# The attention batch of a two-layer block scheduled anew on one Trainium2 core: a third bank for maxima, other banks for the products with values

## The reference

```python
qkv = (x @ w_qkv).reshape(Bx, Tx, 3, H, HD)          # H = 16 heads, HD = 16
q, k, v = ...                                         # each [B, H, T, HD]
scores = jnp.einsum('bhqd,bhkd->bhqk', q, k) * SCALE
scores = jnp.where(causal[None, None], scores, -jnp.inf)
geo_bias = q_proj[..., :, None] * k_proj[..., None, :]
scores = scores + head_scales[None, :, None, None] * geo_bias
attn = jax.nn.softmax(scores, axis=-1)
out = jnp.einsum('bhqk,bhkd->bhqd', attn, v)
return out.transpose(...).reshape(Bx, Tx, Cx) @ w_out
```

## Time and profile before

| | |
|---|---|
| median of three runs | 2681.28 us |
| profiled execution | 2683.27 us, span 2681.3 us |
| mean granted clock of TensorE, whole span | 0.925 |
| TensorE matmuls | 2320.9 us busy, 87% of the span |
| VectorE | 1624.2 us, 61% |
| ScalarE | 1314.3 us, 49% |
| GpSimd | 435.1 us, 16% |
| attention, first to last score product | about 1100 us to 2149 us of the span |

### The profile page before, as it was taken

One profiled execution on the slowest core, in us unless ns is written; L12 is line 12 of the kernel. 1 busy time (PEld: TensorE's weight loads), 2 busy tenths in 40 slices (PEclk: granted clock), 3 DMA queues, 4 the chain that ended last, 5 costly groups with the idle time before them and its releaser, 6 DMA issues. The chain is left out here.

```text
span 2681.3 us, 45165 instructions
## 1 busy us (share of the span) xinstructions
PE 2320.9 (87%) x15010; PEld 1680.5 (63%) x15010; DVE 1624.2 (61%) x3570; ACT 1314.3 (49%) x2260; POOL 435.1 (16%) x364
## 2 busy tenths in 40 slices
PE   7999999998799996588888888888888875169997
PEld 6666667666688884455555555555555565158996
DVE  4666767675444546656666666665666555766664
ACT  3565656564445554555555554555555543034442
POOL 0000000000111114210000000000000022046664
PEclk8999999999899997799989998999999987579998
DMA  4300000000000001232222222332222128145542
GB/s 113 110 0 0 0 0 0 0 0 17 15 0 0 0 0 39 50 81 76 77 71 74 72 73 70 73 76 71 72 72 72 38 92 280 47 130 123 127 93 32
DMA packets 122975, 156.64 MB, mean 58 GB/s; under 512 B 26896, under 2 KB 104096, under 8 KB 122784
## 3 DMA queue, kind: packets, MB, share of 16 engines
q1 hardware_dynamic: 104480, 129.85, 17.7%
q0 software_dynamic: 14336, 25.44, 4.9%
q10 hardware_dynamic: 4096, 0.53, 0.1%
HBM read 96.26 MB, written 58.98 MB: 58 GB/s over the span
## 5 line engine op out<-in xcount | busy, mean ns | idle before, releaser
L1386 DVE TENSOR_REDUCE at_top<-psum 128x1 f32<-128x512 f32 (+3 forms) x1024 | 456.7, 484 | 346.9 <-PE psum L1122 346.6
L1567 ACT ACTIVATE out_x<-psum 128x512 f32<-128x512 f32 (+1 forms) x768 | 385.4, 536 | 449.5 <-PE psum L1140 448.1
L1120 PE MATMUL psum<-out_x 96*128 96x512 bf16 (+3 forms) x1024 | 292.9, 312 | 59.5 <-DVE at_top L1386 42.3
L1138 PE MATMUL psum<-out_x 98*128 98x512 bf16 (+3 forms) x1024 | 289.0, 309 | 60.9 <-DMA out_x<-at_neg_top 37.8
L1122 PE MATMUL psum<-at_mask_q,at_ident_b 128*128 128x128 bf16 x1024 | 205.0, 226 | 0.0
L1120 PEld LDWEIGHTS psum<-out_x 96*128 96x128 bf16 x1024 | 102.6, 100 | 162.4 <-DVE at_top L1386 105.1
L1140 PE MATMUL psum<-at_mask_k,at_ident_b 128*128 128x128 bf16 x1024 | 202.5, 224 | 0.0
L1138 PEld LDWEIGHTS psum<-out_x 98*128 98x128 bf16 x1024 | 101.5, 99 | 159.3 <-issue 70.8
L1156 PE MATMUL psum<-out_x,at_values 128*32 128x512 f32 (+3 forms) x2048 | 165.7, 467 | 0.8 <-ACT out_x L1567 0.8
L2360 POOL DMA_INDIRECT out<-ex_result,slot_tokens x64 | 119.5, 1868 | 102.9 <-DVE ex_result L2492 88.3
L1156 PEld LDWEIGHTS psum<-out_x,at_values 128*32 128x32 f32 x2048 | 64.1, 116 | 94.3 <-issue 79.0
(11 more groups left out here) (400 smaller groups left out, 5896.1 us busy)
## 6 DMA issues: line engine op xcount, KB each, us to landing
out_x<-qk_parts SPq DMA_DIRECT2D x128, 192.0 KB
out_x<-qk_parts SPq DMA_DIRECT2D x128, 128.0 KB
qk_parts<-at_q_parts SPq DMA_DIRECT2D x96, 128.0 KB
qk_parts<-at_k_parts SPq DMA_DIRECT2D x96, 128.0 KB
x_residual<-in_x SPq DMA_DIRECT2D x16, 512.0 KB, 3.9
out_x<-qk_parts SPq DMA_DIRECT2D x128, 64.0 KB
token_rows<-ro_h_tok SPq DMA_DIRECT2D x16, 512.0 KB, 3.0
token_rows<-ro_gate_row SPq DMA_DIRECT2D x16, 512.0 KB, 4.1
```

Of the source, the lines that this page charges most:

```text
L1120: pe.matmul(out, q_stack[0:STACK, h, qt * P:(qt + 1) * P], k_stack[0:STACK, h, 0:w], start=True, stop=True)
L1138: pe.matmul(bank(bk)[:, col:col + w], k_stack[0:STACK + N_SHIFT, h, kt * P:(kt + 1) * P], q_stack[0:STACK + N_SHIFT, h, kt * P:T], start=T ...
L1386: dve.tensor_reduce(top[:, h, qt:qt + 1], bank(MAX0 + n % 2)[:, col:col + w], AX.X, ALU.max).then_inc(mxr.sem, 1)
L1567: act.activation(probs[:, slot(h), 512 * f:512 * f + w], bank(f)[:, 0:w], ACT.Exp).then_inc(ex.sem, 1)
```

## The change

Maxima get a bank for each fill (banks 3, 4 and 6), so a fill waits for the same fill of the head before. The products with values and the turned maxima go to the side banks, chosen by group (`PV_BANK`, `TOP_BANK`), turned outputs always to bank 7 (`O_BANK`), and the two output products and the two turnings back take opposite banks (`OUT_BANK`, `DELTA_BANK`). `oT` has two buffers. q and k products come in the order q, k, q, k, one after each of the heads 0 to 3, v products after heads 5 and 11 instead of both after head 3; other side work moves by a head or so. VectorE negates the maxima after the second fill of a head instead of the third. The row DMAs of maxima move from ScalarE's list to SP's (except the very first). SP stores by halves of the heads with a semaphore for each, and interleaves rows, stores and loads. The core of the diff:

```diff
-        MAX0, SIDE_A, PV_BANK, SIDE_B = 3, 5, 6, 7
+        MAX0, SIDE_A, MAX2, SIDE_B = 3, 5, 6, 7
+        PV_BANK = (SIDE_A, SIDE_A, SIDE_A, SIDE_B)
+        TOP_BANK = (SIDE_A, SIDE_B, SIDE_A, SIDE_A)
+        O_BANK = SIDE_B
+        OUT_BANK, DELTA_BANK = (SIDE_B, SIDE_A), (SIDE_A, SIDE_B)
         HALF_X = NB // 2
...
         MAX_TILES = (((3, 0),), ((2, 0), (0, 384)), ((1, 0),))
+        MAX_BANK, MAX_DONE = (MAX0, MAX0 + 1, MAX2), (1, 3, 4)
...
                 pe.wait_ge(*loaded[h // GROUP](b, loaded[0].per))
-            n = 3 * h + f
-
-            if n >= 2:
-                pe.wait_ge(*mxr(b, 4 * ((n - 2) // 3) + (1, 3, 4)[(n - 2) % 3]))
+            if h:
+                pe.wait_ge(*mxr(b, 4 * (h - 1) + MAX_DONE[f]))
             elif not (isinstance(b, int) and b == 0):
-                pe.wait_ge(*mxr(b - 1, 4 * HEADS - 1 + n))
+                pe.wait_ge(*mxr(b - 1, 4 * (HEADS - 1) + MAX_DONE[f]))
             for qt, col in MAX_TILES[f]:
                 w = (qt + 1) * P
-                out = bank(MAX0 + n % 2)[:, col:col + w]
...
         def pe_batch(pe, i, first, last, turn):
             for h in range(HEADS):
+                g = h // GROUP
+                after = (i, g + 1) if g + 1 < NG else (i + 1, 0)
                 for f in range(3):
                     if f == 2 and h % GROUP == 0 and not (first and h == 0):
-                        pe.wait_ge(*neg(i, N_SHIFT * (h // GROUP + 1)))
-                        pe_pv(pe, *((i, h // GROUP - 1) if h else (i - 1, NG - 1)))
+                        pe_pv_bank_free(pe, i, h, first, last)
+                        pe_pv(pe, *((i, g - 1) if h else (i - 1, NG - 1)))
                     pe_scores(pe, i, h, f, first)
                     if h + AHEAD < HEADS:
                         pe_max(pe, i, h + AHEAD, f)
                     elif not last:
                         pe_max(pe, i + 1, h + AHEAD - HEADS, f)
-                    if f == 1 and h % GROUP == 1 and not (last and h + GROUP > HEADS):
-
-                        g = h // GROUP
-                        if g:
+                    if f == 1 and h % GROUP == 1 and not (last and g == NG - 1):
+                        if h > 1:
                             pe.wait_ge(*oe(i, g))
                         else:
-                            pe.wait_ge(*(neg(i, N_SHIFT) if first else oe(i - 1, NG)))
-                        pe_turn_max(pe, *((i, g + 1) if g + 1 < NG else (i + 1, 0)))
-                if h in (0, 1) and not last:
-                    for n in (2 * h, 2 * h + 1):
-                        if n == 0:
-                            pe.wait_ge(*hTl(i + 1, DK))
-                        elif n >= 2:
-                            pe.wait_ge(*qr(i + 1, n - 1))
-                        pe_qk(pe, n)
-                if h == 3 and not last:
-                    pe.wait_ge(*qr(i + 1, 4))
-                    pe_values(pe, i + 1)
-                if h == 4 and not first:
-                    if not last:
-                        pe.wait_ge(*ve(i + 1, 2))
-                    pe_turn_o(pe, i - 1, 3, SIDE_B)
+                            pe.wait_ge(*(hTf(i + 1, DK) if first else oe(i - 1, NG)))
+                        pe_turn_max(pe, *after)
+                if h == 0 and not last:
+                    pe.wait_ge(*hTl(i + 1, DK))
+                    if first:
+                        pe.wait_ge(*neg(i, N_SHIFT))
+                    pe_qk(pe, 0)
+                if h == 1 and not last:
+                    pe.wait_ge(*neg(i, 2 * N_SHIFT))
+                    pe_qk(pe, 1)
+                if h in (2, 3) and not last:
+                    pe.wait_ge(*qr(i + 1, h - 1))
+                    pe_qk(pe, h)
+                if h == 5 and not last:
+                    pe.wait_ge(*neg(i, 3 * N_SHIFT))
+                    pe_values(pe, i + 1, (0,))
                 if h == 5 and not first:
+                    pe.wait_ge(*(neg(i, 2 * N_SHIFT) if last else qr(i + 1, 4)))
+                    pe_turn_o(pe, i - 1, 3)
+                if h == 6 and not first:
+                    pe.wait_ge(*(neg(i, 3 * N_SHIFT) if last else ve(i + 1, 1)))
                     for f in range(DK):
                         pe_turn_tok(pe, i - 1, f)
-                if h == 7:
-                    pe.wait_ge(*(ve(i + 1, 2) if first else yl(i - 1, 2)))
-                    pe_turn_o(pe, i, 0, SIDE_B)
-                if h == 8 and not first:
+                if h == 8:
+                    pe.wait_ge(*(qr(i + 1, 4) if first else yl(i - 1, 2)))
+                    pe_turn_o(pe, i, 0)
+                if h == 9 and not first:
+                    pe.wait_ge(*on(i, 1))
                     pe_out(pe, i - 1, 0)
-                if h == 9:
+                if h == 10:
                     if not first:
-                        pe.wait_ge(*on(i, 1))
+                        pe.wait_ge(*neg(i, 4 * N_SHIFT))
                         pe_out(pe, i - 1, 1)
-                if h == 10:
-                    pe.wait_ge(*(ve(i + 1, 2) if first else dl(i - 1, 1)))
-                    pe_turn_o(pe, i, 1, SIDE_A)
+                    pe.wait_ge(*(on(i, 1) if first else dl(i - 1, 1)))
+                    pe_turn_o(pe, i, 1)
+                if h == 11:
                     if not first:
                         pe_turn_delta(pe, i - 1, 0)
+                    if not last:
+                        pe.wait_ge(*on(i, 2))
+                        pe_values(pe, i + 1, (1,))
                 if h == 12 and not first:
-                    pe.wait_ge(*xs(i - 1, 1))
+                    pe.wait_ge(*(on(i, 2) if last else ve(i + 1, 2)))
                     pe_turn_delta(pe, i - 1, 1)
                 if h == 13:
-                    pe.wait_ge(*on(i, 2))
-                    pe_turn_o(pe, i, 2, SIDE_A)
+                    pe.wait_ge(*(ve(i + 1, 2) if first else xs(i - 1, 2)))
+                    pe_turn_o(pe, i, 2)
                     if turn:
-                        pe.wait_ge(*(on(i, 1) if first else xs(i - 1, 2)))
-                        pe_turn_ln(pe, i + 2, 1)
+                        pe.wait_ge(*neg(i + 1, N_SHIFT))
+                        pe_turn_ln(pe, i + 2, 1, SIDE_A)
                 if h == 14 and turn:
-                    pe.wait_ge(*on(i, 3))
-                    pe_turn_ln(pe, i + 2, 0)
+                    pe.wait_ge(*hTf(i + 2, 1))
+                    pe_turn_ln(pe, i + 2, 0, SIDE_A)
+
+        def pe_pv_bank_free(pe, i, h, first, last):
+            if h == 0:
+                pe.wait_ge(*on(i - 1, 3))
+            elif h == GROUP:
+                pe.wait_ge(*(neg(i, N_SHIFT) if last else qr(i + 1, 3)))
+            elif h == 2 * GROUP:
+                pe.wait_ge(*(ve(i + 1, 1) if first else yl(i - 1, 1)))
+            else:
+                pe.wait_ge(*(neg(i, 4 * N_SHIFT) if first else xs(i - 1, 1)))
...
                         dve_max(dve, i + 1, h + AHEAD - HEADS, (f,))
-                    if f == 2 and h % GROUP == 1 and not (last and h + GROUP > HEADS):
+                    if f == 1 and h % GROUP == 1 and not (last and h + GROUP > HEADS):
...
-        def sp_store(sp, b, side):
-
-            if side == 0 and not (isinstance(b, int) and b == 0):
-                sp.wait_ge(*loaded[NG - 1](b - 1, loaded[0].per))
-            sp.wait_ge(*q3(b, 2 * side + 2))
+        def sp_store(sp, b, n):
+
+            side, m = n % 2, n // 2
+            later = not (isinstance(b, int) and b == 0)
+            if n == 0 and later:
+                sp.wait_ge(*loaded[1](b - 1, loaded[0].per))
+            sp.wait_ge(*q3(b, n + 1))
+            if n == 2 and later:
+                sp.wait_ge(*loaded[3](b - 1, loaded[0].per))
             for j in range(3):
-                for m in range(2):
-                    sp.dma_start(parts_dram[side, j, :, 8 * m:8 * m + 8, :].rearrange("c h t -> h c t"),
-                                 qk_parts[side][:, j, m, :]).then_inc(stored.sem, 16)
+                sp.dma_start(parts_dram[side, j, :, 8 * m:8 * m + 8, :].rearrange("c h t -> h c t"),
+                             qk_parts[side][:, j, m, :]).then_inc(stored[m].sem, 16)
         def sp_load(sp, b, g):
             if not (isinstance(b, int) and b == 0):
                 sp.wait_ge(*stp(b - 1, 3 * GROUP * (g + 1)))
-            if g == 0:
-                sp.wait_ge(*stored(b, stored.per))
-                if isinstance(b, int) and b == 0:
+            if g % 2 == 0:
...
-        def sp_batch(sp, i):
-            for side in range(2):
-                sp_store(sp, i + 1, side)
-            for g in range(NG):
-                sp_load(sp, i + 1, g)
+        def sp_row(sp, b, g):
+            sp.wait_ge(*neg(b, N_SHIFT * (g + 1)))
+            for j in range(N_SHIFT):
+                sp.dma_start(q_stack[STACK + j:STACK + j + 1, GROUP * g:GROUP * (g + 1), :].rearrange(
+                    "a h (q p) -> a (h q) p", p=P), neg_top[:, j, :]).then_inc(row[g].sem, 16)
+
+        def sp_batch(sp, i, last=False):
+            sp_row(sp, i, 1)
```

(81 more changed lines are left out.)

143 lines of the change are left out of this document (61 added, 82 removed).

## The result

The changed kernel took 2652.67 us (median of four runs, 2648.74 to 2657.10) beside 2681.84 of the kernel before on the same chip: a ratio of 0.9892, 95% interval 0.9868 to 0.9916. It is faster by 29 us, not by the 69 that were forecast. The profiled execution took 2649.17 us, 34.1 less than that of before.

The account below looks back on a forecast made before the run. TensorE was taken as nearest the bound, losing 13.1 of 65.8 us per batch. Per batch 58.8 + 1.5 row wait + 1.0 clock = 61.3, 4.5 less, times 14 = 63; with 7.5 outside, 70 off 2683.3: 2613, range 2565 to 2672.

Parts of the forecast that it names:

- What bounds it: Attention batches: no engine full, TensorE nearest; 13.1 of 65.8 us per batch lost to three kinds of loss.
- (a): Score products at head 8 wait for the DMA of a row of maxima: 2.33 us per batch.
- (b): After the row wait at head 8 TensorE's granted clock is at its lower level: mean loss put at 2.4 us.
- The new order without the row: Per batch 52.7 us of TensorE work plus 6.1 of hand-counted waits: 58.8, before row wait and clock loss.
- Rival C: Third bank does nothing for maxima because VectorE is late: 65.8 us per batch, 2676 in all; chance 0.08.
- q and k by heads, stores by halves: First six stores end 20 us after the batch's first score product (T 20), so load 0 starts then, not at 27.9.
- Rival D: Half the stores take as long as all: load 0 at T 24.1, row wait 6.2 us, slower, 2698; chance 0.12.
- Rows from SP: SP issues row 2 after load 0 and store 2, at T 24.7 to 25.9; head 8 waits 1.5 us.
- late bound: Row 2 lands at T 32.1, after load 0's 9.8 us and then store 2; head 8 then waits 2.1 us.
- The clock: Lower TensorE clock after the row wait at head 8: 0 to 2.4 us per batch, taken as 1.0.
- rival B: Strict ring order in SP's queue: row wait 3.0 us, clock loss 2.4, 64.2 per batch, 2656 in all; chance 0.14.
- Outside batches 1 to 14: Savings of 4.5 us in batch 0, 2 in the last batch, 1 in the seven opening heads: 7.5.

Follow-up runs that it names:

- parts_two_banks: Changed kernel with each load as twelve one-part DMAs and maxima alternating between two banks instead of a bank per fill: 2594.9 us.
- row2_mid: Changed kernel with row 2 in SP's list behind load 0 but ahead of store 2: 2605.2 us.
- rows_act: Changed kernel with the rows of maxima issued by ScalarE again instead of SP: 2599.0 us.
- parts16: Changed kernel with each load as twelve DMAs of one part instead of six of one to three: 2568.4 us.
- parts_neg0: Changed kernel with each load as twelve one-part DMAs and maxima turned and negated after the first fill of heads 1, 5, 9, 13: 2561.8 us.
- before_parts16: Kernel before the change with each load as twelve DMAs of one part instead of six of one to three: 2612.7 us.

## Why the prediction was wrong

*What bounds it* held. The row at head 8 and the clock behind it were named as losses (a) and (b), and are what is left.

*The new order without the row* held. 58.8 per batch were worked out; with the row wait and the clock taken off, the changed kernel has 64.0 - 3.6 - 2.4 = 58.0, and split loads, which leave 0.7 of the wait, ran at 58.6. Most waits counted came as counted: head 1 0.90 (1.0), head 5 1.19 (1.3), the turned output of head 6 0.48 (0.5), head 12 0.77 (0.8). That behind the negations of head 13 was half of it, 0.6 (1.2). All waits of TensorE but that for the row come to 4.4 per batch (62 us in 14), where 6.1 were counted. The total is nearer (58.0 for 58.8) because about 0.9 per batch go in no wait that the view lists; so far it is luck. Of the kernel before the same sum says 65.8 - 2.33 - 2.4 = 61.1, and with split loads it ran at 61.5. Rival C, that the third bank does nothing, is wrong by parts_two_banks: 26 us.

*q and k by heads, stores by halves* held: load 0 at T 20.1 (20). Rival D is out.

*Rows from SP* is the step that failed: when the row lands behind a load and a store. Its issue (T 25.8, within 24.7 to 25.9) and its need (T 29.9 for 30.0) were right. The landing was not: the row came at T 33.5, past the late bound of 32.1, and I had taken a wait of 1.5, "nearest the old row". Two terms of that bound were in the text, load 0's 9.8 and 2.3 for store 2. Measured, the load holds a row for 11.8 (row2_mid) and the store for another 1.6. By the landings in the changed kernel, load 0's last part came 11.0 after its first issue, and the row's last 2.3 later: the store was sized right, the load 1.2 too short. The early bound, a row that lands free in 1.8, was no real case: while load 0 runs, a row was in flight for 5.8 even in a queue of its own (rows_act). The old row, which I took as the nearest, had stood in such a queue, and that is just what the change took from it. So the wait is 3.6 instead of 1.5. That ScalarE loses the issues was put at 0; against rows_act it is worth 1.5 per batch in waits for ScalarE's copies, which the hand count did not have either, so that the sum is not touched by it.

*The clock* was sized to fit the smaller wait: 1.0, with 2.4 as the bound. It was 2.4 in the batch shown and 2.5 as a mean. After row waits of 1.6 at most (rows_act; 1.0 in parts16) the clock stayed at 1.00 over the batches; with 1.8 as a mean (row2_mid) it was 0.98, with 3.6 0.95. The two terms make 2.1 + 1.4 = 3.5 per batch, 49 us in batches 1 to 14; the base was 0.8 better than counted (58.0), 11 us. That leaves 2.7 per batch, the difference between 4.5 and 1.8.

So rival B came true: wait 3.0, clock 2.4, 64.2 per batch and 2656, against 64.0 and 2653. That its number is so near is in part luck, since its wait was 0.6 too short and the base 0.8 too long. Its reason, that in SP's queue a row stands behind a load and a store, is right as far as rows_act shows it (2.5 us); the larger part is the load itself.

By the Trainium skill ("DMA: Bandwidth & Descriptors", Issuing engines are not separate DMA queues) issuing from another engine saves issue time alone. Here the measurement decides otherwise for a small DMA behind a large one: issued 0.6 us sooner, the row landed 2.5 us sooner, 5.8 after its issue instead of 7.7.

*Outside batches 1 to 14* the sum was right in size by accident: 7.5 were forecast, 34.1 - 25.1 = 9.0 came (921.1 less 896.0 lie inside). Batch 0 gave 2.4 and not 4.5 (59.49 to 57.07, from 1119.74 to 1176.81). The opening heads gave 2.5 and not 1, and another 3.1 come from the very first maxima, which the prediction did not cover: they start at 1096.94 against 1100.03, as SP issues the first load 2.8 earlier (1085.65 against 1088.48). Whether stores by halves did that was not tested.

*A larger miss lay in what I took for given.* I priced the tail of a load as given. It was a choice of the kernel, in two lines (LOADS) that the change does not touch: mending it is worth 66 us in the kernel before, the whole change 29 as it stands and 44 with the loads mended.

## What to carry to other kernels

When a small DMA that somebody waits for is moved into another queue, price it by what stands ahead of it there to its last byte, tail included, and don't let its record in the old queue stand for the new one. A tail at which a tenth of the DMA engines is busy can come from the way in which a transfer is cut, as it did here; look for it before reordering around it. Once one wait dominates, other edits look worthless (the third bank 11 us and not 26, earlier negations 8 and not 20): take away the longest wait first, then measure the rest again.

## What the runs showed of the hardware

- The two 4 KB DMAs of a row took up to 7.6 us to land behind a load and a store in SP's list, up to 7.7 from ScalarE's list while a load ran, and 2.3 at most behind a load of twice as many DMAs with the same bytes on its receiving side (parts16). More and smaller DMAs (64 KB each, where the old ones have up to 192) were the faster ones.
- After a wait of 3.6 us the granted clock stood at 0.58 for 6 us, and 32 matmuls of 2.36 us took 3.63. Over the batches, row waits of 1.0 left 1.00, of 1.8 0.98. One run has both: in parts_neg0 head 8 took 4.41 or 4.42 us after each of thirteen row waits of 1.2 to 1.5, and 6.05 after the one of 3.0, in batch 14, where the granted clock was 0.72 over 6 us.
- The clock of before_parts16, 0.98 without a row wait, falls nearly always in one place: in nine of fourteen batches at the end of head 3, behind two waits of about 0.75 and 0.56 us (one of 1.14), for ScalarE and for a reduction of maxima that holds a bank. Head 3 then lasts 8.2 us (1254.93 to 1263.11) instead of 6.6 (1316.94 to 1323.58), about 1.0 per batch as a mean, of the 2.9 that lie between it and the new order with split loads. Not settled is why the same two waits are followed by a fall in some batches and not in others.
